# Found experts' weights loaded on semaphores of their own, in other buffers and at other places in the DMA queue

## Chip, cores and metric

The kernel runs on one core of one Trainium2 chip. The metric is the device time of one execution in microseconds (us). Three executions before the change took 1085.42, 1087.01 and 1088.35 us; the median is 1087.01.

## What is computed

The program is one forward pass of a small perceiver-like stack on a query `x` of 2 batches x 128 positions x 256 features and a context of 2 x 2048 positions. Twelve sublayers follow each other, three in each of four layers: cross attention, self attention or a recurrence, and a feed-forward part. The change lies in the feed-forward part of layer 0, a mixture of experts, and touches the cross attention of layer 1 that follows it:

```python
shared_out = _gated_mlp(x, shared_w1, shared_w3, shared_w2)      # for all 256 tokens
gates = softmax(x @ wg.T)                                        # 16 experts
topk_w, topk_idx = top_k(gates, 2);  topk_w /= sum(topk_w)
combine = zeros((T, 16)).at[rows, topk_idx].set(topk_w)
for w1, w3, w2, cw in the 16 experts:
    acc += cw[:, None] * (silu(x @ w1.T) * (x @ w3.T) @ w2.T)
out = shared_out + acc
```

After it, layer 1 attends with 16 heads from the 128 positions to the 2048 context positions under a mask; the kernel calls that stage the causal one.

## The kernel before

One instruction stream is written by hand for each engine, and the streams meet only in semaphores. SyncE (SP) issues nearly all DMAs in program order; an SP wait holds back all that stands behind it.

**Experts in rounds.** The class `Experts` packs the token-expert pairs into blocks of 32 slots. One round takes four blocks at once, one on each 32-row part of the tensor array; there are 8 rounds (`ROUNDS`), the last with three blocks (`groups`). Rounds 0 to 3 hold the first 32 tokens of each of the 16 experts, so their weights are known in advance: block i uses expert i. Rounds 4 to 7 hold what overflows from the experts that got more than 32 tokens. Which expert each of these 15 blocks needs is found on VectorE (`places`, L833 on), which writes 16 integers to `self.found` and raises the semaphore `l0_hin` to 4. SP then reads a number with `value_load` and issues a load from the address that it gives: the "found" loads.

**Buffers.** An expert's weights are 1536 floats in each of 128 partitions: 1024 for the two up matrices (a load of 512 KB), 512 for the down matrix (256 KB). `HOMES` lists 16 places, one for each of the 16 blocks of four rounds; round t uses those of round t - 4 again. So the up part for round t can be loaded when the up product of round t - 4 is done, and the down part when its down product is done. Places 0 to 3 lie in `vv`, the value tables of the attention; place 14 is the end of `big`, which the shared expert's second block also uses until its down product is done (`block_y` 6); place 15 is the start of `prob`, free when the gate of that block is done (`block_h` 6).

**TensorE's order.** `Experts.tensor` (L707 on) runs a loop of t from 0 to 10: up(t) at L634, in t = 0 also the down product of the shared block, then down(t - 2) at L649, turn(t - 1) at L661, combine(t - 3) at L680 and gather(t + 2) at L671. combine adds the round's result, weighted, to PSUM. The last combine raises `l0_proj` to 14 and 15. Then `Experts.add_last` on VectorE adds the sum to `x`, and the causal stage begins.

**SP's order.** `late_sync` loads experts 10 to 13 and 15 for rounds 2 and 3. `found_sync` then issues, in this order: up 4, expert 14 after `block_y` 6, up 5, up 6, down 4, up 7, down 5, down 6, down 7. Every found load reads its number just before (L545). The semaphores are shared: up loads of rounds 4 and 6 count on `block_in1`, those of 5 and 7 on `w0_in`, all down loads on `block_in2`. So that a count tells which load landed, SP waits at L553 (rounds 6 and 7) and L559 (rounds 5 to 7) until the round before on the same semaphore has landed, before it issues the next.

**The causal stage.** `Causal.sync` (L1858 on) waits for `l0_proj` 14, then loads the split keys of unit u = 2 to 31 (three DMAs each), four value tables of 1020 KB after u = 2, 3, 4 and 5 (`reload_values`, since the experts used their places), and pieces of later stages' weights. Units 0 and 1 have their keys already. TensorE takes two units' scores before the keys of unit 2 are needed. Tables 2 and 3 are read from unit 16 and 24 on. `Causal.prepare` on VectorE (six small operations, the last a clearing of rows in `probT`) runs between the experts' rounds, at t = 4.

GpSimd meanwhile splits the context keys into bf16 parts and writes them to DRAM (`Split.gpsimd`, L1680 on): four of its 16 stores of 384 KB fall into the rounds.

Of the kernel before, what the change touches and what calls it, by code (L numbers as in the profile page):

```python
# [66 lines left out]
EXPERTS, ROUNDS, SLOTS, EXP = 16, 8, 32, 6 * D  # L67
# [20 lines left out]
HOMES += [begin("big") + EXP * i for i in (5, 3, 4, 6, 7)] + [begin("prob")]  # L88
# [428 lines left out]
class Experts:  # L517
# [19 lines left out]

    def load(self, sp, dram, e, sem):
        lo = HOMES[e]
        sp.dma_start(self.k.arena[:, lo:lo + EXP], dram[e]).then_inc(self.k.s(sem), 16)  # L540

    def load_found(self, sp, dram, t, lo, n, sem):
        for g in self.groups(t):
            i = 4 * (t - 4) + g
            e = sp.value_load(self.found[0:1, i:i + 1], min_val=0, max_val=EXPERTS - 1)  # L545
            at = HOMES[i] + lo
            sp.dma_start(self.k.arena[:, at:at + n], dram[bass.ds(e, 1)].rearrange("a p n -> (a p) n")[:, lo:lo + n]).then_inc(self.k.s(sem), 16)

    def load_found_up(self, sp, dram, t):
        sp.wait_ge(self.k.s("block_up"), 6 + t - 3)  # L550
        if t >= 6:
            sem, count = self.UP_LOADED[t - 2]
            sp.wait_ge(self.k.s(sem), count)  # L553
        self.load_found(sp, dram, t, 0, 1024, self.UP_LOADED[t][0])

    def load_found_down(self, sp, dram, t):
        sp.wait_ge(self.k.s("block_y"), 6 + t - 3)
        if t >= 5:
            sp.wait_ge(self.k.s("block_in2"), 64 + 64 * (t - 4))  # L559
        self.load_found(sp, dram, t, 1024, 512, "block_in2")  # L560

    def found_sync(self, sp, dram):
        s = self.k.s
        sp.wait_ge(s("l0_hin"), 4)
        self.load_found_up(sp, dram, 4)
        sp.wait_ge(s("block_y"), 6)
        self.load(sp, dram, 14, "block_in0")
        self.load_found_up(sp, dram, 5)
        self.load_found_up(sp, dram, 6)
        self.load_found_down(sp, dram, 4)  # L570
        self.load_found_up(sp, dram, 7)
        self.load_found_down(sp, dram, 5)
        self.load_found_down(sp, dram, 6)
        self.load_found_down(sp, dram, 7)
# [4 lines left out]
    UP_LOADED = {2: ("l0_in", 48), 3: ("block_in0", 160), 4: ("block_in1", 160), 5: ("w0_in", 96), 6: ("block_in1", 224), 7: ("w0_in", 144)}  # L579
    DOWN_LOADED = {4: 128, 5: 192, 6: 256, 7: 304}  # L580
# [27 lines left out]
    def late_sync(self, sp, dram, early):  # L608
        s = self.k.s
        sp.wait_ge(s("block_y"), 4)  # L610
        self.load(sp, dram, 10, "l0_in")
        early.stored(sp, early.LATE)
        self.load(sp, dram, 11, "l0_in")
        self.load(sp, dram, 12, "block_in0")
        sp.wait_ge(s("block_y"), 5)
        self.load(sp, dram, 13, "block_in0")
        sp.wait_ge(s("block_h"), 6)
        self.load(sp, dram, 15, "block_in0")

    def weight(self, t, g, lo, n):  # L620
        at = HOMES[4 * (t % 4) + g] + lo
        return self.k.arena[:, at:at + n]
# [15 lines left out]
    def down(self, pe, t):  # L638
        k, s = self.k, self.k.s
# [5 lines left out]
        if t >= 4:  # L645
            pe.wait_ge(s("block_in2"), self.DOWN_LOADED[t])
# [194 lines left out]
    def vector(self, dve, o, between):  # L841
# [6 lines left out]
        for t in range(ROUNDS + 1):  # L848
# [6 lines left out]
            if t == 4:  # L855
                between()
# [906 lines left out]
class Causal(Keys):  # L1763
# [91 lines left out]
    def sync(self, sp, later, ctx, found_sync):  # L1855
        k = self.k
        found_sync()
        for slot in range(2):  # L1858
            sp.wait_ge(k.s(f"split_out{slot}"), 8 * len(Split.BLOCKS))
        sp.wait_ge(k.s("l0_proj"), 6 + ROUNDS)  # L1860
        for u in range(2, 32):
# [3 lines left out]
            if u in (2, 3, 4, 5):  # L1865
                self.reload_values(sp, u - 2, ctx)
# [1630 lines left out]
```

## Time and profile before

| | |
|---|---|
| median of three executions | 1087.01 us |
| the profiled execution | 1087.82 us |
| its span, first to last instruction | 1086.0 us |
| mean granted clock of TensorE | 0.985 of full |
| TensorE matmul busy | 1008.1 us, 93% of the span |
| VectorE / ScalarE / GpSimd busy | 703.9 / 501.2 / 238.6 us |
| the experts' rounds on TensorE | 163.7 to 221.6 us of the span |

The page gives the busy time of each engine, the span in 40 slices of 27 us, the DMA queues, the chain of work that ended last, the costliest groups of instructions, and the DMAs by line with their size. A busy TensorE at 93% means that a stage elsewhere can only gain what its own idle time and its slow-clock time hold. The timeline lists merged runs of instructions with the idle time before them and what ended it; the windows give busy time, clock and DMA rate of a chosen stretch.

### The profile page before, as it was taken

Reading aid. Unit: us, or ns where it says so; the run is one execution under the profiler, and the core shown is the slowest. Engines: PE = TensorE matmul, PEld = TensorE weight load, DVE = VectorE, ACT = ScalarE, POOL = GpSimd, SP = SyncE. Lnnn points to the kernel's source line nnn. Section 1 sums busy time; section 2 is a strip of 40 time slices with the busy share of each in tenths; the row PEclk is TensorE's granted clock in tenths of the full one; section 3 lists DMA queues with packets and bytes.
Section 4 is the critical chain, followed back from the end, with each engine's and each line's share of the span. In section 5 each row is a group of like instructions: output and inputs, shape, how many; then the busy total and the mean of one; then the engine's idle time right before and its main releaser. Section 6 shows DMA issues by size and latency. Waiting matters only on the chain.

```text
span 1086.0 us, 23469 instructions
## 1 busy us (share of the span) xinstructions
PE 1008.1 (93%) x9600; PEld 800.5 (74%) x9600; DVE 703.9 (65%) x1352; ACT 501.2 (46%) x889; POOL 238.6 (22%) x361
## 2 busy tenths in 40 slices
PE   8999898788999889999989899999999999999886
PEld 3755674446677547777765789999999999999764
DVE  3746355376886478888545776776666576777466
ACT  3242222245776358888764533433323223332384
POOL 4630527012132000000012511210010133332120
PEclk9999998999999999999999999999999999999997
DMA  9761869667663426000141000131111122100000
GB/s 381 299 235 71 307 241 352 223 195 207 184 160 99 162 79 209 2 2 2 41 155 40 1 1 21 40 117 40 41 58 39 57 63 68 59 21 11 1 2 11
DMA packets 42202, 116.66 MB, mean 107 GB/s; under 512 B 4592, under 2 KB 13296, under 8 KB 40432
## 3 DMA queue, kind: packets, MB, share of 16 engines
q1 hardware_dynamic: 38192, 103.56, 28.4%
q0 software_dynamic: 2752, 9.44, 2.5%
q10 hardware_dynamic: 1152, 2.16, 0.5%
q8 instruction: 76, 1.25, 0.5%
q14 instruction: 30, 0.25, 0.1%
HBM read 99.94 MB, written 15.20 MB: 106 GB/s over the span
## 4 chain that ended last, share of the span: by engine, by line
PE 76%; DVE 12%; issue 4%; ACT 3%; DMA 3%; SPq 1%; POOL 1%; DVEq 0%; ACTq 0%; POOLq 0%
PE ps L2588 11%; PE ps L2545 10%; PE ps L1734 6%; PE ps L2102 6%; PE ps L2443 4%; PE ps L2432 4%; PE ps L440 3%; PE ps L2093 3%; PE ps L1890 3%; PE ps L1901 3%; PE ps L433 3%; PE ps L1397 2%; DMA arena<-experts_in 2%; PE ps L1389 2%; PE ps L1742 1%
## 5 line engine op out<-in xcount | busy, mean ns | idle before, releaser
L2588 PE MATMUL ps<-arena 128*128 128x129 f32 x1024 | 126.6, 276 | 1.7 <-DVE xn L2775 1.7
L2588 PEld LDWEIGHTS ps<-arena 128*128 128x128 f32 x1024 | 119.6, 191 | 2.5 <-ACT arena L2694 2.1
L2028 DVE TENSOR_REDUCE st<-ps 128x1 f32<-128x512 f32 x128 | 82.4, 686 | 22.9 <-PE ps L1890 21.1
L2727 DVE TENSOR_REDUCE probT<-ps 128x128 f32<-128x1024 f32 x64 | 82.6, 1290 | 21.9 <-PE ps L2545 12.8
L2205 DVE CUSTOM_DVE_ANT_0 arena<-ps,arena 128x1024 f32<-128x1024 f32 x64 | 75.8, 1223 | 21.7 <-PE ps L2093 18.4
L2694 ACT ACTIVATE arena<-arena 128x1024 f32<-128x1024 f32 x64 | 71.1, 1111 | 27.4 <-DVE arena L2739 27.4
L2667 ACT COPY w<-ps 128x128 f32<-128x128 f32 x32 | 8.5, 266 | 160.0 <-PE ps L2554 160.0
L1975 ACT ACTIVATE arena<-ps 128x1024 f32<-128x1024 f32 x64 | 65.8, 1030 | 32.8 <-PE ps L1901 31.8
L2739 DVE TENSOR_TENSOR arena<-ps,probT 128x1024 f32<-128x1024 f32 x64 | 79.6, 1286 | 1.1
L2102 PEld LDWEIGHTS ps<-const,arena 128*128 128x128 f32 x512 | 54.8, 141 | 31.5 <-issue 24.3
L170 POOL TENSOR_SCALAR small<-small 128x4 f32<-128x4 f32 (+1 forms) x44 | 13.3, 303 | 285.8 <-DVE small L2482 152.8
L2173 ACT ACTIVATE arena<-arena,st 128x1024 f32<-128x1024 f32 x64 | 73.9, 1155 | 0.0
L2102 PE MATMUL ps<-const,arena 128*128 128x128 f32 x512 | 69.9, 279 | 1.6 <-ACT arena L2157 1.6
L1734 PE MATMUL ps<-arena 128*17 128x128 f32 x2048 | 68.5, 274 | 0.0
L2432 PE MATMUL ps<-arena 128*128 128x128 f32 x512 | 62.4, 276 | 0.7 <-ACT arena L2475 0.7
L2443 PE MATMUL ps<-arena 128*128 128x128 f32 x512 | 62.6, 275 | 0.0
L2545 PE MATMUL ps<-arena 128*128 128x128 f32 x512 | 60.2, 276 | 2.3 <-DVE arena L2739 2.3
L2443 PEld LDWEIGHTS ps<-arena 128*128 128x128 f32 x512 | 60.3, 192 | 2.5 <-issue 2.4
L2545 PEld LDWEIGHTS ps<-arena 128*128 128x128 f32 x512 | 58.5, 192 | 3.8 <-DVE arena L2739 2.2
L2432 PEld LDWEIGHTS ps<-arena 128*128 128x128 f32 x512 | 59.6, 192 | 1.6 <-ACT arena L2475 1.2
L1734 PEld LDWEIGHTS ps<-arena 128*17 128x17 f32 x2048 | 50.5, 97 | 13.6 <-issue 7.8
L2545 PE MATMUL ps<-w,arena 128*128 128x128 f32 x512 | 60.0, 275 | 0.0
(511 smaller groups left out, 2016.8 us busy)
## 6 DMA issues: line engine op xcount, KB each, us to landing
arena<-ctxT_in SPq DMA_DIRECT2D x28, 512.0 KB, 4.1
arena<-experts_in SPq DMA_DIRECT2D x16, 768.0 KB, 6.1
arena<-experts_in SPq DMA_DIRECT2D x15, 512.0 KB, 8.8
key_parts<-w POOLq DMA_DIRECT2D x16, 384.0 KB, 6.6
arena<-key_parts SPq DMA_DIRECT2D x32, 192.0 KB, 3.4
arena<-blocks_in SPq DMA_DIRECT2D x6, 768.0 KB, 19.8
arena<-ctx_in SPq DMA_DIRECT2D x2, 2176.0 KB, 25.3
arena<-early_values SPq DMA_DIRECT2D x4, 1088.0 KB, 11.9
```

What stands on the lines that cost most here:

```text
L1734: last = pe.matmul(self.k.ps[g:g + 17, bank, 0:P], self.values(u, ch), pT[:, ch * P:(ch + 1) * P], start=(ch < 4), stop=(ch + 4 >= MC))
L2028: dve.tensor_reduce(self.mx[:, u % 2, n:n + 1], k.ps[:, n % 2, :], AX.X, ALU.max).then_inc(s("reduced"), 1)
L2102: last = pe.transpose(k.ps[:, bank, ch * P:(ch + 1) * P], self.p[u % 4][:, (4 * n + ch) * P:(4 * n + ch + 1) * P], k.const("ident"))
L2173: act.activation(e, e, ACT.Exp, bias=self.nm[:, u % 2:u % 2 + 1]).then_inc(s("exp"), 1)
L2205: dve.tensor_tensor_reduce(out=self.p[u % 4][:, h * 1024:(h + 1) * 1024], in0=k.bank(2 * h, 1024, 2), in1=self.mask[:, u // 16, h * 1024:( ...
L2432: last = pe.matmul(k.ps[:, bank, t * P:(t + 1) * P], tile[:, c, t * P:(t + 1) * P], self.ctx("wk_ctx", DC)[:, c, h * DH:(h + 1) * DH], sta ...
L2443: last = pe.matmul(k.ps[:, bank, t * P:(t + 1) * P], tile[:, c, t * P:(t + 1) * P], self.ctx("wv_ctx", DC)[:, c, h * DH:(h + 1) * DH], sta ...
L2545: last = pe.matmul(k.ps[:, ch // 4, ch % 4 * P:ch % 4 * P + P], keys[:, ch * P:(ch + 1) * P], q, start=True, stop=True)
L2588: last = pe.matmul(k.ps[:, 7, 0:DH + 1], self.prob(u)[:, ch * P:ch * P + P], v, start=(ch == 0), stop=(ch == MC))
L2694: act.activation(e, e, ACT.Exp).then_inc(s("c3_exp"), 1)
L2727: dve.tensor_reduce(self.largest[:, h * P:(h + 1) * P], bank.rearrange("p (c t) -> p t c", t=P), AX.X, ALU.max).then_inc(s("c3_max"), 1)
L2739: dve.tensor_tensor(self.prob(u)[:, lo:hi].rearrange("p (c t) -> p c t", t=P), k.bank(0, hi, 5)[:, lo:hi].rearrange("p (c t) -> p c t", t= ...
```

## The change

Expert 14 goes to the start of `prob` and expert 15 to the start of `probT`; the function `home` tells the place. Expert 15 is now the first load of `late_sync`, ahead of the wait for `block_y` 4; expert 14 is loaded where 15 was, after `block_h` 6. A round's numbers are read once, ahead of its up load's wait, and kept in registers for its down load. Every round's up and down loads have a semaphore that no other found load uses, and the two waits for the landing of an earlier round are gone. In the queue the down load of round 5 changes places with the up load of round 7. VectorE's `prepare` runs at t = 6 after a wait for `block_y` 10 (down of round 3, the last reader of expert 15), and the value tables 0 and 1 are reloaded right behind the found loads, tables 2 and 3 after units 8 and 12.

```diff
--- before.py
+++ after.py
@@ -85,7 +85,7 @@
 
 HOMES = [begin("vv") + MC * VH * q for q in range(4)] + [begin("w03"), begin("qz") + 512]
 HOMES += [begin("big") + EXP * i for i in range(3)] + [begin("kt") + 2048]
-HOMES += [begin("big") + EXP * i for i in (5, 3, 4, 6, 7)] + [begin("prob")]
+HOMES += [begin("big") + EXP * i for i in (5, 3, 4, 6)] + [begin("prob")]
 
 
 class Cols:
@@ -535,49 +535,53 @@
         self.shifted = k.small[:, 400:432].rearrange("p (r n) -> p r n", n=4)
         self.columns = k.small[:, 432:440]
 
+    def home(self, e):
+        return self.k.probT[:, 0:EXP] if e == EXPERTS - 1 else self.k.arena[:, HOMES[e]:HOMES[e] + EXP]
+
     def load(self, sp, dram, e, sem):
-        lo = HOMES[e]
-        sp.dma_start(self.k.arena[:, lo:lo + EXP], dram[e]).then_inc(self.k.s(sem), 16)
-
-    def load_found(self, sp, dram, t, lo, n, sem):
+        sp.dma_start(self.home(e), dram[e]).then_inc(self.k.s(sem), 16)
+
+    def load_numbers(self, sp, t):
+        numbers = []
         for g in self.groups(t):
             i = 4 * (t - 4) + g
-            e = sp.value_load(self.found[0:1, i:i + 1], min_val=0, max_val=EXPERTS - 1)
-            at = HOMES[i] + lo
-            sp.dma_start(self.k.arena[:, at:at + n], dram[bass.ds(e, 1)].rearrange("a p n -> (a p) n")[:, lo:lo + n]).then_inc(self.k.s(sem), 16)
-
-    def load_found_up(self, sp, dram, t):
+            numbers.append(sp.value_load(self.found[0:1, i:i + 1], min_val=0, max_val=EXPERTS - 1))
+        return numbers
+
+    def load_found(self, sp, dram, t, numbers, lo, n, sem):
+        for g in self.groups(t):
+            block = dram[bass.ds(numbers[g], 1)].rearrange("a p n -> (a p) n")
+            sp.dma_start(self.home(4 * (t - 4) + g)[:, lo:lo + n], block[:, lo:lo + n]).then_inc(self.k.s(sem), 16)
+
+    def load_found_up(self, sp, dram, t, numbers):
         sp.wait_ge(self.k.s("block_up"), 6 + t - 3)
-        if t >= 6:
-            sem, count = self.UP_LOADED[t - 2]
-            sp.wait_ge(self.k.s(sem), count)
-        self.load_found(sp, dram, t, 0, 1024, self.UP_LOADED[t][0])
-
-    def load_found_down(self, sp, dram, t):
+        self.load_found(sp, dram, t, numbers, 0, 1024, self.UP_LOADED[t][0])
+
+    def load_found_down(self, sp, dram, t, numbers):
         sp.wait_ge(self.k.s("block_y"), 6 + t - 3)
-        if t >= 5:
-            sp.wait_ge(self.k.s("block_in2"), 64 + 64 * (t - 4))
-        self.load_found(sp, dram, t, 1024, 512, "block_in2")
+        self.load_found(sp, dram, t, numbers, 1024, 512, self.DOWN_LOADED[t][0])
 
     def found_sync(self, sp, dram):
         s = self.k.s
         sp.wait_ge(s("l0_hin"), 4)
-        self.load_found_up(sp, dram, 4)
-        sp.wait_ge(s("block_y"), 6)
-        self.load(sp, dram, 14, "block_in0")
-        self.load_found_up(sp, dram, 5)
-        self.load_found_up(sp, dram, 6)
-        self.load_found_down(sp, dram, 4)
-        self.load_found_up(sp, dram, 7)
-        self.load_found_down(sp, dram, 5)
-        self.load_found_down(sp, dram, 6)
-        self.load_found_down(sp, dram, 7)
+        four = self.load_numbers(sp, 4)
+        self.load_found_up(sp, dram, 4, four)
+        five = self.load_numbers(sp, 5)
+        self.load_found_up(sp, dram, 5, five)
+        six = self.load_numbers(sp, 6)
+        self.load_found_up(sp, dram, 6, six)
+        self.load_found_down(sp, dram, 4, four)
+        seven = self.load_numbers(sp, 7)
+        self.load_found_down(sp, dram, 5, five)
+        self.load_found_up(sp, dram, 7, seven)
+        self.load_found_down(sp, dram, 6, six)
+        self.load_found_down(sp, dram, 7, seven)
 
     def groups(self, t):
         return range(3 if t == ROUNDS - 1 else 4)
 
-    UP_LOADED = {2: ("l0_in", 48), 3: ("block_in0", 160), 4: ("block_in1", 160), 5: ("w0_in", 96), 6: ("block_in1", 224), 7: ("w0_in", 144)}
-    DOWN_LOADED = {4: 128, 5: 192, 6: 256, 7: 304}
+    UP_LOADED = {2: ("l0_in", 48), 3: ("block_in0", 160), 4: ("block_in1", 160), 5: ("w0_in", 96), 6: ("context_keys0", 80), 7: ("context_keys1", 64)}
+    DOWN_LOADED = {4: ("block_in2", 128), 5: ("quant_in", 80), 6: ("x_const_in", 96), 7: ("block_in0", 208)}
 
     def early_sync(self, sp, dram, moe, early, causal):
         k, s = self.k, self.k.s
@@ -607,6 +611,7 @@
 
     def late_sync(self, sp, dram, early):
         s = self.k.s
+        self.load(sp, dram, 15, "block_in0")
         sp.wait_ge(s("block_y"), 4)
         self.load(sp, dram, 10, "l0_in")
         early.stored(sp, early.LATE)
@@ -615,11 +620,10 @@
         sp.wait_ge(s("block_y"), 5)
         self.load(sp, dram, 13, "block_in0")
         sp.wait_ge(s("block_h"), 6)
-        self.load(sp, dram, 15, "block_in0")
+        self.load(sp, dram, 14, "block_in0")
 
     def weight(self, t, g, lo, n):
-        at = HOMES[4 * (t % 4) + g] + lo
-        return self.k.arena[:, at:at + n]
+        return self.home(4 * (t % 4) + g)[:, lo:lo + n]
 
     def up(self, pe, t):
         k, s = self.k, self.k.s
@@ -643,7 +647,8 @@
         else:
             pe.wait_ge(s("router"), 9)
         if t >= 4:
-            pe.wait_ge(s("block_in2"), self.DOWN_LOADED[t])
+            sem, count = self.DOWN_LOADED[t]
+            pe.wait_ge(s(sem), count)
         for c in range(DC):
             for g in self.groups(t):
                 last = pe.matmul(k.ps[32 * g:32 * g + 32, 4, 0:D], self.hT[t % 2][:, c * P + 32 * g:c * P + 32 * g + 32],
@@ -852,7 +857,8 @@
                 self.gate(dve, t)
             if t >= 1:
                 self.make_give(dve, o, t - 1)
-            if t == 4:
+            if t == 6:
+                dve.wait_ge(self.k.s("block_y"), 6 + 4)
                 between()
 
     def add_last(self, dve, o, b):
@@ -1855,6 +1861,10 @@
     def sync(self, sp, later, ctx, found_sync):
         k = self.k
         found_sync()
+        for q in range(2):
+            sp.wait_ge(k.s("block_y"), 6 + 4 + 1)
+            sp.wait_ge(k.s("block_up"), 6 + 6 + q + 1)
+            self.reload_values(sp, q, ctx)
         for slot in range(2):
             sp.wait_ge(k.s(f"split_out{slot}"), 8 * len(Split.BLOCKS))
         sp.wait_ge(k.s("l0_proj"), 6 + ROUNDS)
@@ -1862,8 +1872,8 @@
             if u >= 4:
                 sp.wait_ge(*self.at("keys_queries", 2 * (u - 3)))
             self.load_keys(sp, u)
-            if u in (2, 3, 4, 5):
-                self.reload_values(sp, u - 2, ctx)
+            if u in (8, 12):
+                self.reload_values(sp, u // 4, ctx)
             if 3 <= u < 3 + len(later):
                 to, source, loaded = later[u - 3]
                 sp.dma_start(to, source).then_inc(k.s(loaded), 16)
```

## Rows read from the trace of the kernel before

**Rows 1.** The page's first line.

```profile
span 1086.0 us, 23469 instructions
```

**Rows 2.** Timeline of TensorE, 175 to 220 us: start, duration, instructions, idle before and its releaser.

```profile
175.42 1.16 PE L671 MATMUL ps<-arena,xn 128*128 128x128 f32 x8 [0.75 <-DVE arena L784]
180.98 3.64 PE L634 MATMUL ps<-arena 128*32 128x512 f32 x16 [4.40 <-DMA arena<-experts_in]
...
188.72 1.92 PE L634 MATMUL ps<-arena 128*32 128x512 f32 x16
...
198.40 1.92 PE L634 MATMUL ps<-arena 128*32 128x512 f32 x16
200.14 1.05 PE L649 MATMUL ps<-arena 128*32 128x256 f32 x16
...
202.35 1.92 PE L634 MATMUL ps<-arena 128*32 128x512 f32 x12
...
205.34 1.03 PE L680 MATMUL ps<-attT,arena 128*128 128x256 f32 x4
211.22 1.93 PE L649 MATMUL ps<-arena 128*32 128x256 f32 x16 [4.86 <-DMA arena<-experts_in]
...
217.01 1.29 PE L649 MATMUL ps<-arena 128*32 128x256 f32 x12 [2.05 <-DMA arena<-experts_in]
218.23 3.40 PE L680 MATMUL ps<-attT,arena 128*128 128x256 f32 x8
```

**Rows 3.** Windows: length, busy us of PE, PEld, DVE, ACT, POOL; PEclk, DMA share, GB/s.

```profile
168.40:178.50 10.10, 7.43 (x69) 3.66 (x68) 8.26 (x16) 2.93 (x8) 7.12 (x8) 1.00 0.97 325
178.50:196.04 17.54, 15.06 (x124) 7.39 (x124) 6.21 (x19) 3.36 (x9) 10.77 (x13) 0.81 1.03 411
...
170.00:174.00 4.00, 4.00 (x46) 2.08 (x42) 3.12 (x6) 1.47 (x4) 3.76 (x5) 1.00 0.95 241
...
180.16:186.98 6.82, 6.00 (x35) 2.10 (x36) 0.42 (x1) 0.76 (x2) 6.00 (x7) 0.50 1.03 416
...
210.88:214.29 3.41, 3.07 (x20) 1.79 (x21) 0.00 (x0) 0.75 (x2) 0.00 (x0) 0.50 0.30 81
217.70:221.12 3.42, 3.42 (x13) 2.36 (x8) 0.00 (x0) 1.86 (x3) 0.00 (x0) 0.50 0.00 0
```

**Rows 4.** The one load issued at 170.94 (expert 14): us from issue to landing.

```profile
DMA to landing us min/median/max: 10.0/10.0/10.0
```

**Rows 5.** Waits of SP's queue: us in total, times, longest.

```profile
SPq L559 <- DMA arena<-experts_in: 9.9, 3, 4.6
```

**Rows 6.** SP's issues of DMAs by size: KB each, median us to landing.

```profile
arena<-experts_in SPq DMA_DIRECT2D x15, 512.0 KB, 8.8
...
key_parts<-w POOLq DMA_DIRECT2D x16, 384.0 KB, 6.6
...
arena<-experts_in SPq DMA_DIRECT2D x15, 256.0 KB, 3.1
```

**Rows 7.** Line 545 on SP, reading a number: duration ns min/median/max.

```profile
L545 SPq TENSOR_LOAD <-small x30: 264/273/615, 165.8 to 213.4; - x30
```

**Rows 8.** Timeline of SP.

```profile
113.86 2.53 SPq L540 DMA_DIRECT2D arena<-experts_in  x5
...
174.72 1.43 SPq L547 DMA_DIRECT2D arena<-experts_in  x2
```

**Rows 9.** The one load issued at 161.51 (expert 15): us to landing.

```profile
DMA to landing us min/median/max: 5.5/5.5/5.5
```

**Rows 10.** Timeline of VectorE: first and last of six operations of prepare, gate 7.

```profile
193.97 0.28 DVE L1729 TENSOR_REDUCE small<-const 128x17 f32<-128x68 f32 x1
...
195.16 0.14 DVE L1792 MEMSET probT<- 128x96 bf16 x1
...
204.74 0.42 DVE L792 TENSOR_TENSOR arena<-arena,ps 128x256 f32<-128x256 f32 x1 [1.00 <-ACT arena L739]
```

**Rows 11.** Causal stage's start on TensorE: scores of unit 2.

```profile
233.44 0.90 PE L1890 MATMUL ps<-arena 96*128 96x512 bf16 x2 [0.60 <-DVE st L2028]
```

## The prediction, made before the changed kernel ran

> **What bounds the kernel now.** I read the page first, then the timeline of TensorE over the experts' rounds, then windows of that stretch, then SP's waits. In a span of 1086.0 us [rows 1] TensorE is the engine to watch, and in the rounds it stands idle for weights three times: 4.40 us ahead of up 3, 4.86 us ahead of down 6, 2.05 us ahead of down 7 [rows 2]. The reader should see that each is released by a DMA from `experts_in`. The windows show a second cost: the granted clock is 0.50 in 180.16 to 186.98, 210.88 to 214.29 and 217.70 to 221.12, behind each idle time, so at 1.2 GHz where the rest runs at 2.4 [rows 3]. Between these places the rounds run without any DMA wait: up 4 starts at 188.72 and up 6 at 198.40, 4.84 us a round; up 7 follows 3.95 us later, since that round gathers nothing more [rows 2].
>
> Why the weights are late: expert 14 was issued at 170.94 and took 10.0 us [rows 4], since it had to wait for the shared block's last product and then stood in a busy queue. At the end it is SP: line 559 waits 9.9 us in three waits for earlier landings [rows 5]. Expert 14 is late with the DMA engines full, the tail is late with them partly idle.
>
> **The change, part by part.**
>
> *Expert 14 in `prob`, 15 in `probT`.* Expert 14 takes 15's place in the queue, issued at about 161.5 and landing 5.5 us later [rows 9], at 167.0. Expert 15 is issued at about 142.5, 0.79 MB or 1.9 us at 411 GB/s, behind the shared block's weights, and round 3 wants it 34 us later: nothing. So up 3 starts when gather 4 ends, 175.42 + 1.16 = 176.6, not at 180.98. With the clock left at full the round takes 4.84 us where it took 188.72 - 180.98 = 7.74. That is 4.4 + 2.9 = 7.3 us. Ideal starts are then 176.6 for up 3, 181.4, 186.3, 191.1 for up 4 to 6 and 195.05 for up 7.
>
> *Semaphores of their own.* SP's waits for landings go. What remains are the waits for a free buffer: up 4 at about 166, up 5 after up 1, up 6 after up 2, down 4, down 5, up 7 after up 3 (178.5), down 6 after down 2 (about 184), down 7 after down 3 (about 189). Ideal tail: from up 7, 206.37 - 202.35 = 4.02 us to the end of combine 4; down 6, turn and combine 5 at 2.21 us (200.14 to 202.35); down 7 with three blocks of four, 0.75, and two combines at 0.96. That is 8.9 us, end at 203.95. Before, the last combine ended at 218.23 + 3.40 = 221.63 [rows 2]. The whole, if every weight is there, is 17.7 us.
>
> *What is late next.* With no wait in SP the DMA engines set the pace. An up load is 0.524 MB, a down load 0.262, a split store of GpSimd 0.393 [rows 6]. To the last byte of up 7 the engines must move four rounds of up loads (15 x 0.524 = 7.86), eight down loads (2.10) and four stores (1.57): 11.53 MB, with down 6 and 7 13.4 MB. I take the stream to run from 168.4, 2.6 us behind the first read at 165.8 [rows 7]. At the 411 GB/s of 178.50 to 196.04, where the DMA share is 1.03, up 7 has landed at 168.4 + 28.1 = 196.5, 1.4 us late. If the first 10.1 us go at 325 GB/s as before [rows 3], it lands at 178.5 + 8.25/0.411 = 198.6, 3.5 us late. Part of that slowness was issue pitch, which falls (below); part was not, as 170 to 174 ran at 241 GB/s with a DMA share of 0.95. I take the middle, 2.5 us. Behind the shortest idle time of before, 2.05 us, the clock fell for 3.4 us [rows 2, 3], a loss of 1.7; I add it. In the slower of the two sums the others come in time: up 4 at 174.9 (wanted 181.4), up 5 181.7 (186.3), up 6 187.7 (191.1), down 4 190.3 (192.9), down 5 193.8 (196.5), down 6 201.1 and down 7 203.1 (202.6 and 204.8 once up 7 has waited).
>
> The Trainium skill's page "DMA: Bandwidth & Descriptors", section "Where 436 GB/s comes from", says that for transfers from HBM to SBUF the HBM side binds, at about 358 GB/s per core. By that figure, as an estimate, up 7 would land at 168.4 + 32.2 = 200.6 and the gain would be 10.4 us. The trace does not agree, since it holds 411 GB/s for 17.5 us [rows 3]; the measurement decides, and no term here uses the figure.
>
> *Numbers read once.* A read costs 0.27 us in the median [rows 7], and two found issues take 1.43 us, a pitch of 1.1; five plain loads take 2.53 us, a pitch of 0.53 [rows 8]. I take 0.53 for a found issue, between 0.5 and 1.1. Fifteen reads go and fifteen stand ahead of the up loads' waits. A 512 KB load takes 1.3 us of the engines, so with either pitch the queue stays full: nothing on the path beyond the rate above. If the pitch stayed at 1.1, the 3.5 us end holds.
>
> *Down 5 ahead of up 7.* Its wait, for down 1, ends at about 179.4, after up 3's end: SP loses about 1 us with some 10 us of loads queued. The swap puts 1.05 MB, 2.6 us, ahead of up 7, which is counted above and is exactly what makes up 7 late; the former order would make down 5 the marginal one.
>
> *`prepare` at t = 6.* Six operations, 193.97 to 195.30, 1.3 us on VectorE. Its new place is between give 5 and gate 7, where VectorE was idle for 1.00 us [rows 10]. Gate 7 may slip 0.3 us; turn 7 wants it only after down 6, over 2 us later. Its new wait (down 3) is over before: zero. Without this cover it costs at most 1.3.
>
> *Value tables.* 0 and 1 are issued after up 6 and up 7, at about 194 and 199, behind all found loads of the same queue, 2.1 MB or 5 us, so on to about 208. Behind the waiting instruction on SP stand only the keys of unit 2, which wait for `l0_proj` 14 anyway. Those keys are wanted at 233.44 [rows 11], 11.8 us after the last combine: cover enough. In that stage VectorE releases TensorE (the same row), not a DMA, so fewer table loads there gain nothing; bounds 0 to 0.5 either way. Tables 2 and 3 come after units 8 and 12 for units 16 and 24: nothing.
>
> **The sum.** 7.3 (expert 14) + 10.4 (tail) - 2.5 (up 7 waits) - 1.7 (clock) = 13.5 us. The profiled execution took 1087.82 us and would take 1074.3; the median of the runs is 0.81 lower, so 1073.5.
>
> **Rivals.**
> 1. *Nothing waits.* The deep queue keeps the full rate from the start. For it: 411 GB/s is held wherever the queue is long. Gain 16.3 (wait of 1.4, no clock loss) to 17.7: 1069.3 to 1070.7.
> 2. *DMA bound at the early rate.* 325 GB/s all through: up 7 lands at 168.4 + 35.5 = 203.9, 8.9 late, with 1.7 for the clock a gain of 7.1: 1079.9. For it: VectorE, GpSimd and DMA were all busy in 168 to 178, and they now overlap through rounds 3 and 4. Against: 416 GB/s with GpSimd busy 6.00 of 6.82 us, though VectorE then did only 0.42. That the tail waits survive in another form costs about the same, since expert 14 alone gives 7.3: 1079.7.
> 3. *Given back.* The causal stage starts early but waits for keys behind 2 MB of tables. It decides only if the queue holds over 11 us of work at the last combine. 1087.0.
> 4. *Slower.* The found loads as one deep queue run at the 241 GB/s of 170 to 174 throughout. The last down load lands at 168.4 + 55.5 = 223.9; with 0.75 + 1.9 of work behind it and 1.7 for the clock the rounds end at 228.3, 6.7 us later than now: 1093.7. It decides below 13.4 MB in 48.8 us, 274 GB/s. Against it stands the 411 of rows 3.
>
> **Numbers.** Forecast 0.61, rival 1 0.13, rival 2 0.17, rival 3 0.04, rival 4 0.05. A measurement of this kernel can tell about 0.3%, 3.3 us, from no change. The forecast and rivals 1 and 2 are faster by more: 0.91; same 0.04 (rival 3); slower 0.05. The range 1068.5 to 1080.0 takes in rivals 1 and 2 with half a us at the fast end.
>
> **What would show it.** Up 3 within 1 us of gather 4 and up 4 near 181.4 of the span; granted clock 1.00 in 180 to 187; a DMA share near 1.0 without a gap from 168 to 201; at most one wait for `experts_in`, ahead of up 7, of 1 to 4 us; the last combine ending near 208; from there to the scores of unit 2 the same 11.8 us. The prediction is wrong if a found load waits on SP for anything but a free buffer, if round 3 or 4 is held by VectorE, if down 6 or down 7 still waits for its weights, or if the stages behind change their length by over 1 us.

## The result: 8 us faster, inside the range, 5 us short of the forecast

Seven executions of the changed kernel took 1074.55 to 1079.97 us, median 1077.11; seven of the kernel before took 1081.55 to 1088.35, median 1085.42. The ratio is 0.9939, with a 95% interval of 0.9918 to 0.9959, so 4.5 to 8.9 us of 1085. The prediction said 1073.5, from 1068.5 to 1080.0, and faster with a chance of 0.91. The gain of the medians is 8.3 us where 13.5 were forecast. The time is 3.6 us above the forecast and not 5.2, since the prediction counted from 1087.01, the median of three executions.

The page's first lines after the change:

```profile
span 1075.7 us, 23419 instructions
## 1 busy us (share of the span) xinstructions
PE 1003.9 (93%) x9600; PEld 797.7 (74%) x9600; DVE 707.2 (66%) x1352; ACT 500.3 (47%) x889; POOL 239.5 (22%) x361
```

The span is 10.3 us below that of [rows 1]. It has fifty instructions fewer. Experiment e9 below, which puts the 15 reads of numbers back, has 46 of them again. The timeline of TensorE (start, duration, instructions, idle before and its releaser) answers to [rows 2]:

```profile
172.26 1.16 PE L676 MATMUL ps<-arena,xn 128*128 128x128 f32 x8 [0.76 <-DVE arena L789]
...
178.19 1.92 PE L638 MATMUL ps<-arena 128*32 128x512 f32 x16
...
182.41 1.16 PE L676 MATMUL ps<-arena,xn 128*128 128x128 f32 x8 [0.20 <-DVE arena L789]
183.50 1.92 PE L638 MATMUL ps<-arena 128*32 128x512 f32 x16
...
188.34 1.92 PE L638 MATMUL ps<-arena 128*32 128x512 f32 x16
...
196.64 2.03 PE L638 MATMUL ps<-arena 128*32 128x512 f32 x9 [4.28 <-DMA arena<-experts_in]
...
205.51 1.99 PE L685 MATMUL ps<-attT,arena 128*128 128x256 f32 x8
```

Up 3 now follows gather 4 at once; up 4 is at 178.19, 5.9 us behind gather 4's start where it was 13.3. One wait for weights is left, 4.28 us ahead of up 7. The windows of the same stretch (length, busy us of PE, PEld, DVE, ACT, POOL; clock, DMA share, GB/s) answer to [rows 3]:

```profile
165.25:175.35 10.10, 9.34 (x93) 4.36 (x96) 8.25 (x16) 2.93 (x9) 6.97 (x8) 1.00 0.97 352
175.35:192.88 17.53, 16.82 (x160) 9.51 (x152) 11.09 (x19) 5.49 (x15) 11.61 (x13) 1.00 1.03 408
192.38:196.64 4.26, 0.00 (x0) 0.00 (x1) 2.12 (x8) 0.00 (x0) 0.00 (x0) 1.00 1.03 400
197.45:200.87 3.42, 3.42 (x25) 1.03 (x19) 0.42 (x1) 0.38 (x1) 0.00 (x0) 0.50 1.06 408
```

The DMA engines are full from 165 to the end of the wait, and behind the wait the clock is at 0.50, 1.2 GHz, for 3.4 us, as forecast. The Trainium skill's bound of about 358 GB/s for transfers between HBM and SBUF ("DMA: Bandwidth & Descriptors", "Where 436 GB/s comes from") is passed here too, with 408 over 17.5 us. GpSimd's stores are among the bytes of that window; the 400 GB/s over the 4.26 us of the wait are loads alone.

**Where the time went.** I cut each span at the start of up 0 and at the end of the last combine. The rounds took 221.63 - 163.73 = 57.9 us before and 207.50 - 160.56 = 46.9 after: 11.0 us less. In this profile 3.2 us more lie ahead of up 0. The kernel before ran there at half clock for 3.4 us, at 13 us of the span, and the changed one did not. Over the thirteen profiles of this document up 0 starts at 160.4 to 163.7 us, so I do not put this part down to the change. And the stages behind the rounds took 868.2 us where they took 864.4: 3.8 us were given back. The place is in the causal stage. From the last combine to the first matmul at L440, which follows that stage, the kernel before took 358.13 - 221.63 = 136.5 us and the changed one 348.66 - 207.50 = 141.2, so the stage alone gave back 4.7 us. TensorE's scores of units 2, 9 and 13 after the change:

```profile
219.35 0.90 PE L1900 MATMUL ps<-arena 96*128 96x512 bf16 x2 [0.60 <-DVE st L2038]
...
247.71 1.01 PE L1900 MATMUL ps<-arena 96*128 96x512 bf16 x2 [4.29 <-issue]
...
266.33 1.01 PE L1900 MATMUL ps<-arena 96*128 96x512 bf16 x2 [3.02 <-issue]
```

and those of units 5 and 6 in the kernel before, two rows on which the prediction did not draw:

```profile
246.00 0.59 PE L1890 MATMUL ps<-arena 96*128 96x512 bf16 x2 [2.10 <-issue]
...
251.35 0.59 PE L1890 MATMUL ps<-arena 96*128 96x512 bf16 x2 [2.07 <-issue]
```

The label "issue" says that the profile names no releaser. SP's timeline after the change names it, with the time to landing of unit 8's and unit 9's key loads beside it (the median of three loads stands in the middle):

```profile
234.68 1.80 SPq L1728 DMA_DIRECT2D arena<-key_parts  x3
236.53 0.42 SPq L1859 DMA_DIRECT2D arena<-ctx_in  x1
236.99 0.43 SPq L1879 DMA_DIRECT2D arena<-factors_in  x1
238.74 1.81 SPq L1728 DMA_DIRECT2D arena<-key_parts  x3
```

```profile
DMA to landing us min/median/max: 3.2/3.5/3.5
```

```profile
DMA to landing us min/median/max: 5.0/5.1/7.6
```

Unit 8's keys land 3.5 us after their issue; then value table 2 is issued at 236.53 and needs 8.1 us; unit 9's keys stand behind it, the last issued at 240.0 lands 7.6 us later at 247.6, and TensorE goes on at 247.71. The slow clock sets in during each of the two waits and lasts beyond it:

```profile
245.24:252.07 6.83, 4.36 (x36) 2.97 (x40) 2.14 (x4) 2.21 (x3) 0.00 (x0) 0.50 0.39 85
265.72:272.55 6.83, 6.22 (x58) 3.99 (x59) 2.73 (x5) 2.52 (x5) 0.38 (x2) 0.50 0.39 105
```

### The profile page after: what moved, and what is told of

Read it like the earlier page. It is cut to its first block, busy times and chain, and to the rows that moved or that the text cites. A ratio compares the mean times of both kernels' runs of the same rounds, so it can differ in the third digit from the quotient of the medians.

```text
span 1075.7 us, 23419 instructions
## 1 busy us (share of the span) xinstructions
PE 1003.9 (93%) x9600; PEld 797.7 (74%) x9600; DVE 707.2 (66%) x1352; ACT 500.3 (47%) x889; POOL 239.5 (22%) x361
## 4 chain that ended last, share of the span: by engine, by line
PE 65%; DVE 11%; issue 3%; ACT 2%; SPq 2%; DMA 1%; POOL 1%; ACTq 0%; POOLq 0%; DVEq 0%
PE ps L2598 11%; PE ps L2555 10%; PE ps L1740 6%; PE ps L2112 6%; PE ps L2453 4%; PE ps L2442 4%; PE ps L1900 3%; PE ps L2103 3%; PE ps L1911 3%; PE ps L433 2%; PE ps L1748 1%; DMA arena<-experts_in 1%; SPq L554 1%; PE ps L2462 1%; DVE arena L2749 1%
## 5 line engine op out<-in xcount | busy, mean ns | idle before, releaser
L170 POOL TENSOR_SCALAR small<-small 128x4 f32<-128x4 f32 (+1 forms) x44 | 13.3, 303 | 285.6 <-DVE small L2492 152.8
```

## Experiments

Times are medians; ratios are against the kernel before on the same chip. "Rounds" and "rest" are the two parts of the profiled span as above, rest from the last combine to the end; "causal" is the part of the rest up to L440. Medians of e1 to e4, of e5, e6, e7 and e9, and of e8, e10 and e11 come from three chips, on which the kernel before took 1083.9, 1084.3 and 1084.9 us.

| kernel | us | ratio (95%) | rounds | rest | causal |
|---|---|---|---|---|---|
| before | 1085.4 | | 57.9 | 864.4 | 136.5 |
| changed | 1077.1 | 0.9939 (0.9918 to 0.9959) | 46.9 | 868.2 | 141.2 |
| tables all early (e1) | 1068.0 | 0.9856 (0.9826 to 0.9886) | 46.6 | 860.3 | 133.3 |
| before + homes alone (e2) | 1081.9 | 0.9970 (0.9952 to 0.9989) | 56.7 | 865.1 | 138.1 |
| changed, homes undone (e3) | 1077.0 | 0.9947 (0.9927 to 0.9966) | 46.8 | 865.6 | 140.2 |
| changed, tables back (e4) | 1074.7 | 0.9912 (0.9883 to 0.9940) | 46.9 | 864.1 | 137.1 |
| e1 + up 7 first (e5) | 1065.2 | 0.9821 (0.9801 to 0.9840) | 44.3 | 857.0 | 130.0 |
| e1 + small stores (e6) | 1062.9 | 0.9797 (0.9781 to 0.9813) | 41.8 | 857.0 | 131.1 |
| e1 + kept warm (e7) | 1065.0 | 0.9820 (0.9801 to 0.9839) | 45.9 | 856.1 | 130.2 |
| e1 + a read per load (e9) | 1068.1 | 0.9838 (0.9818 to 0.9859) | 48.6 | 857.8 | 130.8 |
| before + tables early (e8) | 1078.3 | 0.9948 (0.9927 to 0.9969) | 58.9 | 857.2 | 131.8 |
| e5 + kept warm (e10) | 1065.3 | 0.9823 (0.9795 to 0.9850) | 44.0 | 859.1 | 132.3 |
| e6, homes undone (e11) | 1064.8 | 0.9825 (0.9797 to 0.9852) | 43.2 | 858.4 | 131.3 |

**Value tables ahead of the keys.**

```diff
         for q in range(2):
             ...
             self.reload_values(sp, q, ctx)
+        for q in range(2, 4):
+            sp.wait_ge(k.s("block_h"), 6 + 6 + q - 1)
+            self.reload_values(sp, q, ctx)
...
-            if u in (8, 12):
-                self.reload_values(sp, u // 4, ctx)
```

Tables 2 and 3 also count on `block_in1` and `block_in2`, since they are in flight together with 0 and 1.

> The changed kernel, with value tables 2 and 3 also loaded ahead of the keys of unit 2 (right behind tables 0 and 1), not after units 8 and 12. Theory A (a 1020 KB table in the queue ahead of the next unit's keys makes them late; this took 4.3 us at unit 9 and 3.0 us at unit 13, and the slow clock behind each): both waits go, no other comes, since keys of unit 2 have 11.8 us of cover and the tables need 5; the time falls by 6 to 9 us against the changed kernel, to about 1069.5. Theory B (the keys' own rows are slow to read and the waits at units 9 and 13 are theirs): the waits stay, the time stays within 1.5 us of 1077.

Measured 1068.0, 9 us below the changed kernel. Two windows of the causal stage in it, the first over the clock times of unit 9's wait in the changed kernel, whose own window follows in a fence for comparison:

```profile
235.00:247.70 12.70, 12.35 (x214) 8.93 (x214) 10.28 (x21) 9.42 (x17) 2.82 (x12) 1.00 0.70 190
247.70:272.00 24.30, 22.47 (x374) 16.50 (x373) 18.95 (x38) 16.13 (x27) 3.91 (x20) 1.00 0.67 179
```

```profile
235.00:247.70 12.70, 8.42 (x154) 6.27 (x153) 7.40 (x16) 6.61 (x12) 2.70 (x11) 0.90 0.96 256
```

TensorE works 12.35 of 12.70 us where it worked 8.42, and the clock stays at full. The longest wait for keys left in the stage is 1.3 us. Theory A holds. The next two experiments ask the same of the kernel before, and of the tables' old places in the changed kernel.

**The same from the other side: tables alone, on the kernel before.**

```diff
         found_sync()
+        for q in range(4):
+            sp.wait_ge(k.s("block_y"), 6 + 4 + 1)
+            sp.wait_ge(*((k.s("block_up"), 6 + 6 + q + 1) if q < 2 else (k.s("block_h"), 6 + 6 + q - 1)))
+            self.reload_values(sp, q, ctx)
...
-            if u in (2, 3, 4, 5):
-                self.reload_values(sp, u - 2, ctx)
```

> The kernel before, with only the four value tables moved from behind units 2 to 5 to ahead of the keys of unit 2. Its found loads end at about 217 us, so the tables (4.2 MB, 10 us) run until about 228 and the keys of unit 2 behind them are wanted at 233.4. Theory A (a table ahead of a unit's keys makes them late): the waits of 2.1 us each at units 5 and 6 go, with a part of the 3.4 us of slow clock: 4 to 6 us faster than before, about 1079. Theory B (these waits are the keys' own): unchanged, 1084.

Measured 1078.3, 6.6 us below its own kernel before, with the old buffers, semaphores and order of the found loads. Its rounds are 1.0 us longer than before (58.9), its rest 7.2 us shorter, of which 4.7 lie in the causal stage, within the 4 to 6 forecast. The other 2.5 lie behind that stage, where nothing was changed; the kernel before ran at half clock there for 6.8 us at 1067.6, which this one did not. Theory A again. By the ratios, 0.9948 and 0.9939, this one move is worth about as much as the whole change.

**Tables where they were, with the rest of the change.** The edit takes the loop of two out, and puts `if u in (2, 3, 4, 5): self.reload_values(sp, u - 2, ctx)` back.

> The changed kernel with all four value tables after units 2, 3, 4 and 5, as before the change. Theory A (tables ahead of keys make them late, and the later position costs more than the earlier): waits of about 2 us each at units 5 and 6 as in the kernel before, in place of 4.3 and 3.0; 2 to 4 us faster than the changed kernel, about 1074. Theory C (the differences in the causal stage are the chance of a run, the clock's above all): same as the changed kernel within 1 us.

Measured 1074.7, 2.4 us below the changed kernel, which the ratios' intervals do not tell apart. The rounds are unchanged at 46.9, and the rest is 4.1 us shorter, with waits of 2.7 and 1.6 us at units 5 and 6 in place of 4.3 and 3.0. Theory A. Over all profiles the rest is 856.1 to 860.3 with all tables early (eight kernels), 864.1 to 865.1 with tables behind units 2 to 5 (three), 865.6 and 868.2 with tables behind 8 and 12 (two). The groups do not overlap, though the last two differ by little. The causal stage alone parts them more clearly: 130.0 to 133.3, 136.5 to 138.1, and 140.2 and 141.2.

**Expert 14 and 15's places alone.**

```diff
-HOMES += [begin("big") + EXP * i for i in (5, 3, 4, 6, 7)] + [begin("prob")]
+HOMES += [begin("big") + EXP * i for i in (5, 3, 4, 6)] + [begin("prob")]
...
-        self.load(sp, dram, 15, "block_in0")
+        self.load(sp, dram, 14, "block_in0")
```

> The kernel before, with only the buffers of experts 14 and 15 changed (and prepare at t = 6, which the new buffer needs). The prediction's sum counted 7.3 us for this. Theory A (terms add): 7 us faster than before, 1078.5. Theory B (the found loads are a chain of their own on SP and the DMA queue; TensorE arrives earlier and waits longer for down 6 and down 7): only the 1.9 us that expert 14's bytes stood in front of them are gained, and a part of the clock; 2 to 3 us faster than before, with the wait ahead of down 6 grown from 4.9 to about 9 us.

`home()`, the first load of `late_sync` and `prepare` at t = 6 are as in the change; the found loads are as before it. The time fell by 2.0 us. TensorE's waits for weights in it:

```profile
191.54 1.07 PE L648 MATMUL ps<-arena 128*32 128x256 f32 x16 [1.21 <-DMA arena<-experts_in]
195.26 1.92 PE L633 MATMUL ps<-arena 128*32 128x512 f32 x12 [1.42 <-DMA arena<-experts_in]
198.99 1.07 PE L648 MATMUL ps<-arena 128*32 128x256 f32 x16 [1.82 <-DMA arena<-experts_in]
205.91 1.94 PE L648 MATMUL ps<-arena 128*32 128x256 f32 x16 [4.61 <-DMA arena<-experts_in]
212.10 1.93 PE L648 MATMUL ps<-arena 128*32 128x256 f32 x12 [1.93 <-DMA arena<-experts_in]
```

The 4.4 us ahead of up 3 are gone, and come back as three new waits of 4.5 us together ahead of the two old ones. There is not one wait of 9 us, as I had written, but in its sum this is theory B: the rounds are 1.2 us shorter, not 7.3.

**The whole change without these places.** The edit is the reverse: old `HOMES`, expert 14 loaded between up 4 and up 5.

> The changed kernel with the old buffers and the old load of expert 14 between the up loads of rounds 4 and 5 (semaphores of their own, numbers read once, order and tables as changed). Theory A (terms add): 7.3 us slower than the changed kernel, 1084. Theory B (11.5 MB of loads and stores set the start of up 7; waiting in round 3 only uses time that would be waited ahead of up 7): up 3 waits 4 to 5 us, up 7 waits little or not at all, the end of the rounds is 1 to 3 us later than in the changed kernel (expert 14's 1.9 us of queue), 1078 to 1080.

```profile
177.10 3.64 PE L639 MATMUL ps<-arena 128*32 128x512 f32 x16 [2.38 <-DMA arena<-experts_in]
...
199.50 1.49 PE L639 MATMUL ps<-arena 128*32 128x512 f32 x9 [1.27 <-DMA arena<-experts_in]
```

Measured 1077.0, the same as the changed kernel, and the rounds the same, 46.8. TensorE waits 2.4 us ahead of up 3, works round 3 at half clock, and waits 1.3 ahead of up 7 instead of 4.3. Theory B. My 1 to 3 us for expert 14's bytes are there, but hidden: up 7 begins 199.50 - 161.86 = 37.6 us behind up 0, 1.6 later than in the changed kernel. Behind its short wait the clock then stays at full, where the changed kernel runs 3.4 us at half, and that gives the 1.6 back.

**Fewer bytes ahead of up 7.**

```diff
+            m = 512 if n < self.BEFORE_EXPERTS else 64
-            pool.dma_start(self.scratch[b * DC + c].rearrange("a p m -> p a m")[:, :, i * 512:i * 512 + 512], part).then_inc(s(f"split_out{n % 2}"), 16)
+            pool.dma_start(self.scratch[b * DC + c].rearrange("a p m -> p a m")[:, :, i * 512:i * 512 + m], part[:, :, 0:m]).then_inc(s(f"split_out{n % 2}"), 16)
...
-        src = self.scratch[u // 8]
+        src = self.scratch[min(u // 8, 2)]
```

> The e1 kernel, but GpSimd's last four stores of split keys (those inside the rounds) write 64 of 512 columns, and units 24 to 31 of the causal stage read the keys of units 16 to 23; so 1.4 MB leave the stretch ahead of up 7 and the key parts of the last quarter are left out. Theory A (the DMA engines' bytes set when up 7 may start): 1.4 MB at about 400 GB/s is 3.4 us, the wait of 4.1 us ahead of up 7 falls to 0.5 to 1.5, and without the idle time the clock stays up: 3 to 5 us faster than e1, 1063 to 1065. Theory B (the latency of each found load, 8 to 12 us from issue to landing, is the found loads' own, and SP's issues come too late): the wait stays above 3 us, the time within 1 us of e1.

This kernel and the next leave out the key parts of the last quarter, so they are probes and no candidates.

```profile
194.88 1.49 PE L638 MATMUL ps<-arena 128*32 128x512 f32 x9 [0.67 <-DMA arena<-experts_in]
```

The wait ahead of up 7 fell from 4.13 to 0.67 us, by 3.5 for 1.4 MB, and the time to 1062.9. The clock stayed at full. This is theory A: the bytes set the wait.

**The same, with the old places.** The edits of the two experiments together.

> The kernel with small stores (e6: stores of 64 columns, units 24 to 31 read the keys of units 16 to 23, so the key parts of the last quarter are left out) with the old buffers of experts 14 and 15 and the old load of 14 between up 4 and up 5. Question: what the buffers are worth once the bytes ahead of up 7 are fewer. Theory A (the later of two chains sets the start of up 7: TensorE's rounds, 36.4 us from up 0 to up 7 with the old buffers, and the bytes, 34.5): the rounds take 45 us against 41.8 in e6, 3 to 4 us slower than e6, 1066 to 1067. Theory B (the buffers are worth their full 7.3 us when the bytes are away): 1070. Theory C (they are worth nothing, as in e3): 1063.

The rounds take 43.2 us and the time is 1064.8. That is 1.4 us longer than e6 in the rounds and 1.9 in the time, less than any theory but C said. On two chips and with overlapping intervals, the 1.9 is weaker evidence than the 1.4.

```profile
174.95 1.92 PE L639 MATMUL ps<-arena 128*32 128x512 f32 x16 [1.23 <-DMA arena<-experts_in]
...
194.85 1.49 PE L639 MATMUL ps<-arena 128*32 128x512 f32 x9 [1.34 <-DMA arena<-experts_in]
```

The wait for expert 14 is itself 1.23 us here, 2.38 in e3 and 4.40 before. The load asks for the same product each time, the shared block's last, but that is not what it waited for. TensorE's and SP's timelines of the kernel before:

```profile
165.58 1.99 PE L476 MATMUL ps<-arena 128*128 128x256 f32 x8
```

```profile
166.74 4.15 SPq L547 DMA_DIRECT2D arena<-experts_in  x4
170.94 0.43 SPq L540 DMA_DIRECT2D arena<-experts_in  x1
```

The product ends at 167.57, while SP is busy with up 4, a read before each load, until 170.89; expert 14 is issued right behind. In e3 the numbers are read ahead and up 4's issues take 2.05 us, not 4.15. Expert 14 is then issued 5.18 us behind up 0, not 7.21, and lands 10.0 us later in both: the 2.0 us by which the wait is shorter are SP's reads. In e11, with fewer bytes around it, the load lands after 9.0 us, and the wait is shorter again. Theory A had taken TensorE's arrival at up 7 from e3 with e3's wait and slow clock in it, which is why its 3 to 4 us were too many: up 7 begins 34.0 us behind up 0 here. In e6 it begins at 32.6, where the expectation had 34.5 for the bytes.

**Order of the last loads.** `load_found_up(7)` ahead of `load_found_down(5)` again.

> Base is the kernel with all four value tables ahead of the keys (e1_tables_early), 1068.0 us. Here the up load of round 7 stands ahead of the down load of round 5, as before the change. Theory A (the bytes ahead of both set the pace): up 7 lands about 2.6 us earlier, down 5 where up 7 landed; the wait of 4.1 us ahead of up 7 splits into 1.5 ahead of up 7 and 1 to 1.5 ahead of down 5; the rounds end 0.5 to 1.5 us earlier. Theory B (what stands last in the order is all that counts): the wait ahead of up 7 falls by 2.6 and nothing else waits, 1065.

```profile
195.63 1.92 PE L638 MATMUL ps<-arena 128*32 128x512 f32 x12 [2.25 <-DMA arena<-experts_in]
198.44 1.07 PE L654 MATMUL ps<-arena 128*32 128x256 f32 x16 [0.89 <-DMA arena<-experts_in]
201.15 1.07 PE L654 MATMUL ps<-arena 128*32 128x256 f32 x16 [0.41 <-DMA arena<-experts_in]
```

There are three short waits for one of 4.13, 3.55 us in sum, and no slow clock behind them: the rounds take 44.3 us, 2.3 less than in e1. Theory A for the waits; what I had left out was that with these shorter waits the clock stayed at full. The median is theory B's 1065, but its mechanism fails, since down 5 and down 6 wait too. In this profile the swap that the change made costs 2.3 us of the rounds. Against e1 the medians, on two chips, differ by 2.8 us.

**Matmuls that fill the wait.**

```diff
+            if t == ROUNDS - 1:
+                keep_warm(self.k, pe, 16, 2)
```

> The e1 kernel with 16 bf16 matmuls of 512 columns into a free bank ahead of up 7, which fill 3.5 us of the 4.1 us of waiting. Theory A (the slow clock behind the wait, 0.50 for 3.4 us in both profiles so far, comes from TensorE's idle time): the clock stays at full behind it and the rounds end 1.5 us earlier, 1066.5. Theory B (the clock falls with something else): it falls all the same, time within 0.5 us of e1.

```profile
193.00:198.60 5.60, 4.02 (x22) 1.73 (x23) 2.12 (x8) 0.07 (x1) 0.00 (x0) 1.00 1.03 401
198.60:202.00 3.40, 3.40 (x33) 1.59 (x34) 0.42 (x1) 0.97 (x3) 0.00 (x0) 1.00 1.07 412
```

With TensorE busy for most of the wait, the clock behind it is 1.00, not the 0.50 of e1. That is theory A in kind. In size, the rounds are 0.7 us shorter, not 1.5, since up 7 landed 0.8 us later in this execution; most of the 3 us between the medians lies outside the rounds, where the edit changes nothing.

> The e1 kernel with the up load of round 7 ahead of the down load of round 5 (as e5_up7_first) and 8 bf16 matmuls of 512 columns ahead of up 7. e5 already kept the full clock in the rounds (its waits were 2.25, 0.89 and 0.41 us), so the warm matmuls have nothing to give back: rounds as in e5, time 1065 within 1 us. If e7's gain (3 us against e1) came from the warm matmuls and not from the chip it ran on, this one should show 2 us or more against e5.

Measured 1065.3, the same as e5, so the warm matmuls are worth nothing on top of it; e5 had no slow clock in the rounds that they could give back. Some 1 to 4 us between e1 and the later kernels is in the rest and shows in kernels that differ from e1 only in the rounds. The traces show where: up to the end of the causal stage TensorE's scores wait for keys 5.5 us in nine waits in e1, 2.6 in six in e5, 2.9 in five in e7 and 4.5 in eight in e10, each at most 1.3. Why these short waits differ, by chip or by execution, stays open.

**A read ahead of every found load.** `value_load` back inside `load_found`, no `load_numbers`.

> The e1 kernel, but SP reads an expert's number anew ahead of every found load, as before the change (30 reads, a pitch of about 1.1 us an issue where it is 0.5). Theory A (the DMA queue is behind, so SP's pitch costs nothing): up 7 lands within 1 us of where it does in e1, the time within 1 us of 1068. Theory B (a faster pitch is what filled the queue from the start): the queue has gaps in the first 10 us, up 7 lands 2 to 3 us later, 1070 to 1071.

```profile
191.72 1.07 PE L652 MATMUL ps<-arena 128*32 128x256 f32 x16 [1.21 <-DMA arena<-experts_in]
198.22 2.78 PE L636 MATMUL ps<-arena 128*32 128x512 f32 x9 [4.19 <-DMA arena<-experts_in]
```

The profile leans to theory B: there is a wait of 1.21 us ahead of down 4 that e1 does not have, up 7 begins 37.0 us behind up 0 where it was 35.9, about 1 us later and not 2 to 3, and the rounds are 2.0 us longer. The median, 1068.1, sides with A, and the ratios' intervals overlap, 0.9818 to 0.9859 against 0.9826 to 0.9886. The cost is 0 to 2 us and not settled.

## Why the prediction was right, and where its sum was wrong

*What bounds the rounds: right but for expert 14.* There were three waits for weights and three stretches of half clock, with SP's waits for landings behind the last two waits. One wait and one stretch are left. What the prediction said of expert 14, that it had to wait for the shared block's last product, was misread: that product was done 3.4 us before the issue, and SP's reads and issues of up 4 stood in front.

*The wait that is left: right place, mis-sized.* It was forecast ahead of up 7, 2.5 us, with 1.7 for the clock; it is 4.28, with the 3.4 us at 0.50. Up 7 was wanted 31.8 us behind up 0, near the forecast's 195.05 - 163.73 = 31.3; the half us is round 4, which VectorE held (0.20 us ahead of gather 6 in the timeline above). It began at 36.1, forecast 33.8. The stream began when I said, 4.7 us behind up 0, and ran at 352 and 408 GB/s, between my two rates and close to the faster. What I had too low is the bytes: 31.3 us at the measured 389 GB/s are 12.2 MB and not 11.5. Of these, 10.54 MB went through SP's queue, where the loads up to up 7 are 9.96 MB, so some 0.6 MB of later loads had moved before up 7 had landed. The 16 DMA engines do not finish together: the last of them ends a load while others are already on down 6. Time to landing shows it, too. Up 7's three loads took 11.0, 11.0 and 12.4 us, so the last of them, issued at 184.16, landed at 196.6; the first load of down 6, issued behind it at 184.68, took 11.5 and landed at 196.2.

```profile
DMA to landing us min/median/max: 11.0/11.0/12.4
```

Experiment e6 shows that bytes set this wait; how much of the excess is engines apart was read, not tested.

*7.3 us for expert 14: wrong as a term.* I had added it to a tail of 10.4 and then subtracted the new wait, so the sum came out near (13.5 forecast, 11.0 in the rounds), but the part has no such worth: 1.2 us in the rounds alone (e2), 0 on top of the rest (e3), 1.4 with fewer bytes (e11). What the place does change is the start of up 7, by 1.6 us in e3 and 1.4 in e11, near the 1.9 us that expert 14's 0.79 MB need at 411 GB/s; in e3 the clock gave it back. The two chains, TensorE's rounds and the bytes of the queue, run side by side, and up 7 starts with the later. The end of the rounds was in effect forecast from the bytes ahead of up 7, and so it came out near although the split was wrong: the tail's 10.4 less 2.5 and 1.7 leaves 6.2 us, and e3 gained 57.9 - 46.8 = 11.1 without the new places. That gain is that of semaphores of their own, without SP's waits, and of the numbers read ahead. How it divides between the two was not tested on the kernel before.

*"Numbers read once": nothing* may have been 1 to 2 us too low (e9), unsettled. *"Down 5 ahead of up 7"*: its 2.6 us were counted inside the wait, but "the former order would make down 5 the marginal one" hid what the clock does: it stayed at full over three waits of 2.25 us and less in e5 and fell behind one of 4.13 in e1. The length of a wait alone does not decide it, since in the kernel before it fell behind 2.05 us. The swap costs 2.3 us in the rounds (e5). *`prepare` at t = 6*: nothing waited for it, as said; TensorE stood in the wait for up 7 meanwhile.

*The value tables: the step that failed.* "In that stage VectorE releases TensorE (the same row), not a DMA, so fewer table loads there gain nothing" rested on one row at unit 2; at units 5 and 6 the kernel before waited 2.10 and 2.07 us for keys behind a table. And "Tables 2 and 3 come after units 8 and 12 for units 16 and 24: nothing" asked only when the tables are read, not what stands behind them in the queue. Unit 9's keys did, and the measured price of the two tables' new place is 4.7 us of the causal stage. A unit's keys are issued less than 5 us before they are wanted (238.74, and wanted at 247.71 - 4.29 = 243.42), and a table takes 5 to 8. Rival 3 had the right mechanism in the wrong place: it looked at tables 0 and 1, which had their 11.8 us of cover (219.35 - 207.50 = 11.85 again), and not at 2 and 3. Of the 13.5 us, 2.5 are missing in the rounds and 2 to 5 were given back here; 8.3 is what the medians show.

*The range and the signs.* One of the prediction's own signs of being wrong came true: the stages behind changed their length by over 1 us, by 3.8. Round 4 was held by VectorE, another of them, but for half a us. That the time fell inside the range all the same is luck in part. The upper end was there for the slow DMA rate of rival 2, which did not come, and it happened to cover a cost that was put at nothing. It is luck, too, that the last combine ended near 208, at 207.50: in this profile the rounds started 3.2 us earlier than before, and they took 2.5 us longer than forecast.

## What to carry to other kernels

When the loads of one queue are served nearly in the order of their issue, as here, the price of a load that is moved is paid by what stands behind it: look up how long before its use the next small load is issued, and keep large ones away from places where that is less than the large one's time. Waits that are cut in front of a full DMA queue do not add up (7.3 us read from the trace for expert 14 were worth 0 to 2 us of the time); compute when each chain reaches the meeting point and take the later. The best kernel here is not the changed one, but that with all four tables ahead of the keys and up 7 ahead of down 5, 1065.2 us, 0.9821 of before. Keeping down 5 first and filling the wait with matmuls (e7, 1065.0) is not told apart from it.

## What the runs showed that I had not expected

SP's issue of a found load mostly took 0.33 to 0.5 us while few loads were in flight (one of the first nineteen took more, 0.81). From 180.6 on, with some twelve in flight, six of eleven took 0.69 to 1.49. The row of the changed kernel (duration ns min/median/max) shows both ends:

```profile
L554 SPq DMA_DIRECT2D arena<-experts_in x30: 332/364/1492, 163.7 to 189.9; - x30
```

Nothing waited for it, as the engines were full. The keys' loads, 16 to 48 rows each, land in 3.2 to 3.5 us in the median of the kernel before; with one 256 KB piece of later weights beside each unit they hold the DMA engines at a share of 0.67 to 0.70 for 179 to 190 GB/s (the windows of e1), where the weights' loads move 400 at a share of 1.03: by these rows the causal stage's mix of loads takes nearly half as much engine time again for a byte. That this is why a table in front of the keys hurts so soon was not tested.
